# Second cross attention from halves, scores two rows ahead of the values; float8 weight quantised among the experts; rotary tables loaded and widened apart from the masks

## The chip, the core and the metric

One core of a Trainium2 chip runs the whole kernel in one launch. The metric is the device time in microseconds (us), lower is better. In the profile the engines are PE (TensorE matmuls), PEld (its weight loads), DVE (VectorE), ACT (ScalarE), POOL (GpSimd) and SPq (the queue of DMA issues of SyncE).

## The reference

The input x is 8 rows (batch) x 100 tokens x 512 features. Two decoder layers follow each other. Layer 0: a causal self attention with rotary positions (16 heads of 32), a cross attention to a context of 8 x 722 x 512, a mixture of 8 experts with three layers each. Layer 1: a self attention with a latent key and value, a second cross attention to the same context, and one 512 x 512 product with both factors rounded to float8. After each of the six parts the part's input is added and a layer norm taken. The parts that the change touches:

```
q, k = rope(q), rope(k)                     # layer 0: Y*cos + Y2*sin, tables by position
scores = einsum('bqh,bkh->bqk', q, k) * SCALE   # layer 1, second cross attention
attn = softmax(scores, axis=1)              # over the queries, not over the keys
out = einsum('bqk,bkh->bqh', attn, v)
k_q = (kernel / s_k).astype(float8_e4m3fn)  # layer 1, last product
```

## The kernel before

Each stage is a block in which every engine has its own list of instructions, in the order written, and waits on semaphores by hand. A stage ends when all engines have ended it. There is no planner.

**Front (`front_stage`, from L569).** The input rows x and the weights Wq, Wk, Wv, Wo are transposed on PE into PSUM banks, ACT keeps the high half of each result (rounded to fp32r, L693), DVE the low half (L731), and the projections of q and k are made of three products of halves. The list `FRONT` sets one order for all engines: four rows of x, the biases, four chunks of Wq, then sixteen "ropes" (a projected piece of 128 x 400), with the rest of x and of the weights between them. For a rope, PE projects, ACT adds the bias column (L702), POOL multiplies by the cosine table (L722), DVE swaps half heads (L738), multiplies by the widened sine table (L740) and adds (L744). POOL first issues 9 DMAs for biases (L714) and 13 for tables and masks (`rest`, L716: causal, turned_mask, own_chunk, enter, cos, sin, cos_q, sin_q, picks, spreads, gate_w, gate_b, iota8) and waits for all of `rest`. DVE calls `widen_tables` ahead of the low half of the first Wq chunk: it waits for all of `rest` too, then widens four masks (L748 to L751) and two sine tables (L753). SP clears the experts' rows in DRAM (14.8 MB, L626) once `rest` is there.

**Experts (L2035 to L2235).** 60 units (20 tiles x 3 layers) of 16 matmuls each, PE throughout. SP streams one weight of 1 MB per unit into six slots, with the last gathers and a list `last` of other loads between them. DVE has short work in two of three units.

**Second cross attention (`context_columns`, L1478).** Eight rows b, each with its context of 722 keys (6 tiles of 128, the last of 82). The context comes in two layouts: as columns (`ctx_ct`, 1444 KB a row, stored to DRAM by the first cross attention, `load_turned`) for the scores, and as rows in one of five buffers (`load_context`: one DMA of 5 x 128 keys, 1280 KB, and one of the 82 keys left, 164 KB) for the values. Per row: `scores(b)`, 24 float32 matmuls (L1513), keys on the partitions; DVE adds the key bias (L1580), reduces the maximum over the queries (L1586), ACT takes the exponent (L1552), DVE sums (L1596), inverts and multiplies (L1600), which gives `pT`; `value(b, c)`, 24 float32 matmuls with the context as the stationary operand (L1525), which gives the output already turned; 6 small matmuls (12 records) count the sums of `pT` (L1535). ACT copies the output (L1558), DVE the sums (L1606). On PE `scores(b + 1)` stands ahead of `value(b)`. DVE also does one of eight pieces of the float8 rounding of the last weight per row (`kernel_piece`, L2858 and L1171 to L1177). SP waits for scores(b - 2) ahead of the columns of row b; the rows of row b wait for value(b - 5).

The first cross attention (`context_rows`, L1189) already works from halves: ACT rounds the context rows to high halves (L1358), POOL makes the low ones (L1405), and each value is 18 matmuls of 512 columns (L1310).

## Time and profile before

| | us |
| --- | --- |
| median of 3 runs | 1012.65 (1008.77 to 1012.96) |
| the profiled execution: time | 1012.64 |
| the profiled execution: span in the trace | 1010.3 |
| mean granted TensorE clock, share of full | 0.951 |

PE is busy for 930.5 us of the span, DVE for 430.5, ACT for 346.4, POOL for 249.8. What lies around the span (2.3 us) is taken as fixed. A busy share is a mean over stages, so each stage is read in its own stretch: the front ends at about 72 us, the experts run from 447 to 681 us, the second cross attention from 850 to 942 us.

### The profile page before, as it was taken

Reading aid. Unit: us, or ns where it says so; the run is one execution under the profiler, and the core shown is the slowest. Engines: PE = TensorE matmul, PEld = TensorE weight load, DVE = VectorE, ACT = ScalarE, POOL = GpSimd, SP = SyncE. Lnnn points to the kernel's source line nnn. Section 1 sums busy time; section 2 is a strip of 40 time slices with the busy share of each in tenths; the row PEclk is TensorE's granted clock in tenths of the full one; section 3 lists DMA queues with packets and bytes.
Section 4 is the critical chain, followed back from the end, with each engine's and each line's share of the span. In section 5 each row is a group of like instructions: output and inputs, shape, how many; then the busy total and the mean of one; then the engine's idle time right before and its main releaser. Section 6 shows DMA issues by size and latency. Waiting matters only on the chain. (4 is left out here: it accounts for less than half of the span.)

```text
span 1010.3 us, 19157 instructions
## 1 busy us (share of the span) xinstructions
PE 930.5 (92%) x7712; PEld 750.3 (74%) x7712; DVE 430.5 (43%) x994; ACT 346.4 (34%) x886; POOL 249.8 (25%) x306
## 2 busy tenths in 40 slices
PE   3999999989998979999999999998978899999993
PEld 3987776577775643679999999996865568999531
DVE  2884443314443548001121133226257731555576
ACT  2332222234553123112233233325366621212374
POOL 4343111113555207000000000005056503000275
PEclk9999999999999969899999999997969999999996
DMA  9975000246731907049999888711050022972001
GB/s 258 382 257 189 2 2 2 68 128 223 249 138 62 339 1 257 12 140 389 357 382 340 278 272 281 257 39 55 1 156 3 2 96 89 325 241 76 1 14 51
DMA packets 72456, 162.01 MB, mean 160 GB/s; under 512 B 4132, under 2 KB 5685, under 8 KB 70321
## 3 DMA queue, kind: packets, MB, share of 16 engines
q1 hardware_dynamic: 70048, 156.54, 45.3%
q0 software_dynamic: 2320, 4.25, 1.4%
q8 instruction: 61, 1.00, 0.4%
q14 instruction: 27, 0.21, 0.1%
HBM read 128.81 MB, written 31.97 MB: 159 GB/s over the span
## 5 line engine op out<-in xcount | busy, mean ns | idle before, releaser
L2100 PE MATMUL ps<-ffn_h,ffn_w 128*128 128x128 f32 x1280 | 149.1, 275 | 0.0
L2100 PEld LDWEIGHTS ps<-ffn_h,ffn_w 128*128 128x128 f32 x1280 | 145.9, 192 | 0.0
L2100 PE MATMUL ps<-ffn_xh,ffn_w 128*128 128x128 f32 x640 | 74.9, 275 | 0.3 <-ACT ffn_xh L2134 0.3
L2190 DVE TENSOR_SCALAR ffn_h<-ps,tile_bias 128x128 f32<-128x128 f32 x80 | 22.5, 345 | 122.4 <-PE ps L2100 122.4
L2100 PEld LDWEIGHTS ps<-ffn_xh,ffn_w 128*128 128x128 f32 x640 | 73.1, 192 | 0.9 <-issue 0.9
L1405 POOL TENSOR_TENSOR ctx_low<-shelf,ctx_high 128x1024 fp32r<-128x1024 f32 (+2 forms) x24 | 43.0, 1821 | 65.4 <-PE ps L1270 33.7
L2148 ACT ACTIVATE ffn_y<-ffn_y 128x128 f32<-128x128 f32 x80 | 23.7, 298 | 73.9 <-DVE ffn_y L2206 73.9
L2206 DVE SCALAR_TENSOR_TENSOR ffn_y<-ps,tile_bias,ffn_gate_row 128x128 f32<-128x128 f32 x80 | 22.6, 345 | 58.0 <-PE ps L2100 57.9
L1513 PE MATMUL ps<-x_qT,ctx_ct 128*128 128x100 f32 (+1 forms) x384 | 44.8, 278 | 2.3 <-PEq L137 2.0
L1513 PEld LDWEIGHTS ps<-x_qT,ctx_ct 128*128 128x128 f32 (+1 forms) x384 | 43.3, 191 | 3.7 <-issue 3.2
L2818 POOL TENSOR_TENSOR att_e<-att_e,decay 100x400 f32<-100x400 f32 x32 | 32.7, 1033 | 45.8 <-DVE att_e L2669 45.8
L111 PE MATMUL ps<-ctx_ct,x_qT 128*100 128x210 f32 (+1 forms) x128 | 40.3, 467 | 1.0 <-DVE ctx_ct L1419 0.7
L2142 ACT ACTIVATE ffn_h<-ps,tile_bias 128x128 f32<-128x128 f32 x80 | 22.9, 368 | 41.6 <-PE ps L2100 41.6
L2987 POOL TENSOR_TENSOR rstd<-rstd,minus_half 100x1 f32<-100x1 f32 x16 | 11.7, 740 | 97.9 <-DVE rstd L2930 93.3
L111 PEld LDWEIGHTS ps<-ctx_ct,x_qT 128*100 128x100 f32 x128 | 20.6, 166 | 18.7 <-issue 17.4
L1525 PE MATMUL ps<-ctx_pT,shelf 128*128 128x100 f32 (+1 forms) x288 | 33.2, 275 | 0.2 <-ACT xf L1558 0.2
L2765 ACT ACTIVATE att_e<-att_e,att_mx 100x100 f32<-100x100 f32 x96 | 28.0, 366 | 15.4 <-DVE att_mx L2674 15.4
L1525 PEld LDWEIGHTS ps<-ctx_pT,shelf 128*128 128x128 f32 (+1 forms) x288 | 32.6, 192 | 0.4 <-issue 0.4
L1552 ACT ACTIVATE ctx_pk<-ctx_pk,ctx_st 128x100 f32<-128x100 f32 x48 | 13.8, 365 | 53.3 <-DVE ctx_st L1588 53.3
L2890 PE MATMUL ps<-x_n,xf 128*100 128x512 f32 x64 | 29.9, 596 | 0.6 <-PEq L1494 0.6
L111 PE MATMUL ps<-l_ro,xf 128*100 128x512 f32 x64 | 30.1, 615 | 0.0
L2134 ACT ACTIVATE ffn_xh<-ps 128x512 f32<-128x512 f32 x20 | 11.8, 598 | 49.0 <-PE ps L2061 49.0
(467 smaller groups left out, 2092.9 us busy)
## 6 DMA issues: line engine op xcount, KB each, us to landing
ffn_w<-in_L_ffn_w_dram SPq DMA_DIRECT2D x60, 1024.0 KB, 6.5
shelf<-in_ctx_dram SPq DMA_DIRECT2D x12, 1280.0 KB
expert_rows<-nothing SPq DMA_DIRECT2D x1, 14820.0 KB, 51.5
context_turned<-ctx_ct SPq DMA_DIRECT2D x8, 1444.0 KB, 7.9
ctx_ct<-context_turned SPq DMA_DIRECT2D x8, 1444.0 KB, 13.9
ctx_lent<-in_ctx_dram SPq DMA_DIRECT2D x4, 1280.0 KB
rows_own<-expert_rows SPq DMA_DIRECT2D x8, 260.0 KB, 3.0
x_wo<-in_L_xattn_Wo_dram SPq DMA_DIRECT2D x1, 2048.0 KB, 8.4
```

The costliest lines, as they stand in the source:

```text
L111: last = pe.matmul(out, a, b, start=(n == 0), stop=(n == len(products) - 1))
L1405: nc.gpsimd.tensor_tensor(raw_low[b % RAWS][0:rows_, j0:j1, :], raw[b % RAWS][0:rows_, j0:j1, :], raw_high[b % 2][0:rows_, j0:j1, :].bitca ...
L1513: mm = nc.tensor.matmul(ps[0:rows_, SB + i, (j - j0) * T:(j - j0 + 1) * T], ct[b % 2][:, k, j * P:j * P + rows_], qT[:, k, b * T:(b + 1) * T],
L1525: mm = nc.tensor.matmul(ps[:, VB, c * T:(c + 1) * T], raw[b % RAWS][0:keys(j), j, c * P:(c + 1) * P], pT[0:keys(j), b % 2, j, :], start=j ...
L2100: mm = nc.tensor.matmul(acc(n)[:, m, :], w[:, n % SLOTS, k, m * P:(m + 1) * P], into[l][:, i % 2, k, :], start=k == 0, stop=k == C - 1, sk ...
L2142: nc.scalar.activation(h1[:, i % 2, m, :], acc(n)[:, m, :], ACT.Relu, bias=bsel[:, m, i, 0:1]).then_inc(h1_kept, 1)
L2148: nc.scalar.activation(y[:, i % 2, m, :], y[:, i % 2, m, :], ACT.Relu, accum_out=vT[:, m, i:i + 1]).then_inc(counted, 1)
L2190: nc.vector.tensor_scalar(h2[:, i % 2, m, :], acc(n)[:, m, :], bsel[:, m, i, 1:2], 0.0, ALU.add, ALU.max).then_inc(h2_kept, 1)
L2206: nc.vector.scalar_tensor_tensor(y[:, i % 2, m, :], acc(n)[:, m, :], bsel[:, m, i, 2:3], gate_row[:, i % 2, :], ALU.add, ALU.mult).then_in ...
L2765: ins = nc.scalar.activation(e[:, c, :], e[:, c, :], ACT.Exp, bias=mx[:, b % 2, r, c:c + 1])
L2818: nc.gpsimd.tensor_tensor(e, e, decay[:, :].unsqueeze(1).to_broadcast([T, C, T]), ALU.mult).then_inc(faded, 1)
L2890: mm = nc.tensor.matmul(ps[0:T, b % 3, :], xf[:, k, b * T:(b + 1) * T], n1[:, k, :], start=k == 0, stop=False)
```

## The change

**Front.** The four rotary tables get a semaphore of their own and are issued ahead of the masks. POOL waits for them alone. DVE widens the sines at the first rope, and the masks (with the wait for `rest`) at rope 7.

```diff
         rest = [(causal_f, g["causal"]), (turned_f, g["turned_mask"]), (own_chunk[:, 0:C], g["own_chunk"]),
-                        (enter_f, g["enter"].rearrange("p (i r) t -> p i (r t)", i=2)), (cos[:], g["cos"]), (sin[:], g["sin"]), (cos_q[:], g["cos_q"]),
-                        (sin_q[:], g["sin_q"]), (picks[:], g["picks"]), (spreads[:], g["spreads"]),
+                        (enter_f, g["enter"].rearrange("p (i r) t -> p i (r t)", i=2)), (picks[:], g["picks"]), (spreads[:], g["spreads"]),
         in_rest = (in_rest[0], 16 * len(rest))
+        tables = [(sin_q[:], g["sin_q"]), (cos_q[:], g["cos_q"]), (sin[:], g["sin"]), (cos[:], g["cos"])]
+        in_tables = (nc.alloc_semaphore(name="in_tables"), 16 * len(tables))
...
                 def _(pool):
                     for dst, src in loads:
                         pool.dma_start(dst, src).then_inc(in_bias[0], 16)
+                    for dst, src in tables:
+                        pool.dma_start(dst, src).then_inc(in_tables[0], 16)
                     for dst, src in rest:
                         pool.dma_start(dst, src).then_inc(in_rest[0], 16)
-                    pool.wait_ge(*in_rest)
+                    pool.wait_ge(*in_tables)
...
-                    def widen_tables():
+                    def widen_masks():
                         dve.wait_ge(*in_rest)
...
+
+                    def widen_sines():
+                        dve.wait_ge(*in_tables)
                         for i, t in enumerate((sin_q, sin)):
-                            nc.vector.tensor_copy(by_batch(sines[:, i, :]), table(t)).then_inc(masked, 1)
-                        dve.wait_ge(masked, 6)
+                            nc.vector.tensor_copy(by_batch(sines[:, i, :]), table(t)).then_inc(widened, 1)
+                        dve.wait_ge(widened, 2)
...
                     for u in FRONT:
-                        if u == ("wq", 0):
-                            widen_tables()
+                        if u == ("rope", 0):
+                            widen_sines()
+                        if u == ("rope", 7):
+                            widen_masks()
```

On DVE, the front from the low halves of x on. Before:

```order
L731 TENSOR_TENSOR xT_lo<-ps,xT_hi 128x4x100 x4
L731 TENSOR_TENSOR l_bv_lo<-ps,l_bv_hi 128x4
L748 CAST causal<-k_roped 100x400
L750 CAST mask_and_max<-k_roped 128x400 x2
L751 CAST enter<-k_roped 128x400
L753 COPY rope_sines<-sin_q 128x400
L753 COPY rope_sines<-sin 128x400
L731 TENSOR_TENSOR l_wq_lo<-ps,l_wq_hi 128x512 x4
L738 STREAM_SHUFFLE rope_t_55<-rope_f 128x400
```

With the change:

```order
L734 TENSOR_TENSOR xT_lo<-ps,xT_hi 128x4x100 x4
L734 TENSOR_TENSOR l_bv_lo<-ps,l_bv_hi 128x4
L734 TENSOR_TENSOR l_wq_lo<-ps,l_wq_hi 128x512 x4
L759 COPY rope_sines<-sin_q 128x400
L759 COPY rope_sines<-sin 128x400
L741 STREAM_SHUFFLE rope_t_55<-rope_f 128x400
L743 TENSOR_TENSOR rope_t_55<-rope_t_55,rope_sines 128x400
L747 TENSOR_TENSOR q_roped<-rope_t_54,rope_t_55 128x400
```

The four mask casts are gone from ahead of the Wq low halves; the two sine copies stand behind them. The casts now stand in front of the rotation of rope 7.

**Float8 weight.** The load of the weight and of its scale moves from SP's list of the second self attention to the end of the experts' list; the eight pieces move to DVE's list in every second unit from unit 27 on.

```diff
+        in_kernel, k_step = nc.alloc_semaphore(name="in_kernel"), sem("kernel_step")
+        kernel_rows = kq[:].rearrange("p (c d) -> p c d", c=C)
+        PIECE_AT = {unit_at[10, 0] + 2 * b: b for b in range(B)}
+
+        def kernel_piece(dve, b):
+
+            v_, m_ = k_tmp[0][:], k_tmp[1][:]
+            piece = kq[:, b * PIECE:(b + 1) * PIECE]
+            steps = [lambda: nc.vector.tensor_scalar(v_, piece, sc_k[:, 1:2], None, ALU.mult)]
+            steps += float8_steps(piece, v_, m_)
+            for n, emit in enumerate(steps):
+                dve.wait_ge(k_step, len(steps) * b + n + 1)
+                emit().then_inc(k_step, 1)
+
...
-                        (rq, natural(g["L1_attn_Wq"]), in_qup)]
+                        (rq, natural(g["L1_attn_Wq"]), in_qup),
+                        (kernel_rows, natural(g["L1_ffn_kernel"]), in_kernel),
+                        (sc_k[:, 0:1], g["L1_ffn_kernel_scale"].partition_broadcast(P), in_kernel)]
...
+                    if n in PIECE_AT:
+                        b = PIECE_AT[n]
+                        if b == 0:
+                            dve.wait_ge(in_kernel, 32)
+                            nc.vector.reciprocal(sc_k[:, 1:2], sc_k[:, 0:1]).then_inc(k_step, 1)
+                        kernel_piece(dve, b)
```

**Second cross attention.** Values from halves, outputs turned back by PE, three buffers instead of five, scores two rows ahead.

```diff
-        RAWS = 5
+        RAWS, OWN_RAWS = 5, 3
...
-            raw = raws
+            raw = own_raws
+            raw_low = [sb_at(f"{name}_low{i}", [P, KT, D], shelf_at + 4 * KT * D * i, FR) for i in range(OWN_RAWS)]
+            raw_high = [sb_at(name + "_high0", [P, KT, D], xT_at, FR), sb(name + "_high1", [P, KT, D], FR, phase)]
+            pp = Pair(*(sb(f"{name}_pT_{half}", [P, 2, KT, T], FR, phase) for half in ("hi", "lo")))
+            an = sb(name + "_a", [T, 2, D], F32, phase)
...
                 @block.sync
                 def _(sp):
                     for b in range(2, B):
-                        if b >= RAWS:
-                            sp.wait_ge(used, b - RAWS + 1)
-                        load_context(sp, 1, b)
                         sp.wait_ge(scored, 2 * (b - 1))
                         load_turned(sp, b)
+                        if b >= OWN_RAWS:
+                            sp.wait_ge(used, b - OWN_RAWS + 1)
+                        load_context(sp, 1, b)
...
-                    def value(b, c):
-                        if c == 0:
-                            pe.wait_ge(even, b + 1)
-                            pe.wait_ge(landed[b % RAWS], 32 * (b // RAWS + 1))
-                            if b >= 1:
-                                pe.wait_ge(a_kept, b)
+                    def value(b):
+                        pe.wait_ge(low_p, b + 1)
+                        if b >= 1:
+                            pe.wait_ge(natural_a, b)
                         for j in range(KT):
-                            mm = nc.tensor.matmul(ps[:, VB, c * T:(c + 1) * T],
-                                                  raw[b % RAWS][0:keys(j), j, c * P:(c + 1) * P],
-                                                  pT[0:keys(j), b % 2, j, :], start=j == 0, stop=j == KT - 1,
+                            pe.wait_ge(low_raw, len(PIECES) * b + (j // 2 + 1 if j < KT - 1 else len(PIECES)))
+                            r = slice(0, keys(j))
+                            products = times(pp[r, b % 2, j, :], Pair(raw_high[b % 2], raw_low[b % OWN_RAWS])[r, j, :])
+                            for n, (p_, c_) in enumerate(products):
+                                mm = nc.tensor.matmul(ps[0:T, VB, :], p_, c_, start=j == 0 and n == 0,
+                                                      stop=j == KT - 1 and n == 2)
+                        mm.then_inc(used, 1)
+                        if b >= 1:
+                            pe.wait_ge(counted, b)
+                        for j in range(KT):
+                            group = j % HPC
+                            mm = nc.tensor.matmul(ps[group * HD:(group + 1) * HD, 5, 0:T], one[0:keys(j), :],
+                                                  pT[0:keys(j), b % 2, j, :], start=j < HPC, stop=j + HPC >= KT,
                                                   skip_group_check=True)
-                        if c == C - 1:
-                            mm.then_inc(used, 1)
-                            if b >= 1:
-                                pe.wait_ge(counted, b)
-                            for j in range(KT):
-                                group = j % HPC
-                                mm = nc.tensor.matmul(ps[group * HD:(group + 1) * HD, 5, 0:T], one[0:keys(j), :],
-                                                      pT[0:keys(j), b % 2, j, :], start=j < HPC, stop=j + HPC >= KT,
-                                                      skip_group_check=True)
-                            mm.then_inc(summed, 1)
+                        mm.then_inc(summed, 1)
...
+                    def turn_out(b):
+                        pe.wait_ge(natural_a, b + 1)
+                        if b >= 2:
+                            pe.wait_ge(out_kept, b - 1)
+                        for c in range(C):
+                            mm = nc.tensor.transpose(flip_bank(b)[:, c, :], an[:, b % 2, c * P:(c + 1) * P], ident[0:T, 0:T])
+                        mm.then_inc(flipped, 1)
 
                     scores(0)
+                    scores(1)
                     for b in range(B):
-                        if b + 1 < B:
-                            scores(b + 1)
-                        for c in range(C):
-                            value(b, c)
+                        if b + 2 < B:
+                            scores(b + 2)
+                        if b:
+                            turn_out(b - 1)
+                        value(b)
+                    turn_out(B - 1)
...
+                    def split(b, pieces):
+                        for i, rows_, j0, j1 in (PIECES[n] for n in pieces):
+                            if i == 0:
+                                act.wait_ge(landed[b % OWN_RAWS], 32 * (b // OWN_RAWS + 1))
+                                if b >= 2:
+                                    act.wait_ge(used, b - 1)
+                            nc.scalar.activation(raw_high[b % 2][0:rows_, j0:j1, :], raw[b % OWN_RAWS][0:rows_, j0:j1, :],
+                                                 ACT.Identity).then_inc(high_raw, 1)
...
-                    def keep_a(b):
+                    def high_of_p(b):
+                        act.wait_ge(even, b + 1)
+                        if b >= 2:
+                            act.wait_ge(used, b - 1)
+                        nc.scalar.activation(pp.hi[:, b % 2], pT[:, b % 2], ACT.Identity).then_inc(high_p, 1)
+
+                    def keep_natural(b):
                         act.wait_ge(used, b + 1)
-                        nc.scalar.activation(aT_out[:, :, b * T:(b + 1) * T],
-                                             ps[:, VB, 0:C * T].rearrange("p (c t) -> p c t", c=C),
-                                             ACT.Identity).then_inc(a_kept, 1)
-
+                        if b >= 2:
+                            act.wait_ge(flipped, b - 1)
+                        nc.scalar.activation(an[:, b % 2, :], ps[0:T, VB, :], ACT.Identity).then_inc(natural_a, 1)
+
+                    def keep_out(b):
+                        act.wait_ge(flipped, b + 1)
+                        nc.scalar.activation(aT_out[:, :, b * T:(b + 1) * T], flip_bank(b), ACT.Identity).then_inc(out_kept, 1)
+
+                    split(0, range(4))
                     expo(0)
+                    high_of_p(0)
+                    expo(1)
                     for b in range(B):
+                        if b:
+                            keep_natural(b - 1)
                         if b + 1 < B:
-                            expo(b + 1)
-                        keep_a(b)
+                            high_of_p(b + 1)
+                            split(b + 1, range(4))
+                        if b:
+                            keep_out(b - 1)
+                        if b + 2 < B:
+                            expo(b + 2)
+                    keep_natural(B - 1)
+                    keep_out(B - 1)
...
+                    def low_of_raw(b, pieces):
+                        for i, rows_, j0, j1 in (PIECES[n] for n in pieces):
+                            dve.wait_ge(high_raw, len(PIECES) * b + i + 1)
+                            nc.vector.tensor_tensor(raw_low[b % OWN_RAWS][0:rows_, j0:j1, :], raw[b % OWN_RAWS][0:rows_, j0:j1, :],
+                                                    raw_high[b % 2][0:rows_, j0:j1, :].bitcast(F32), ALU.subtract
+                                                    ).then_inc(low_raw, 1)
...
+                    low_of_raw(0, (0, 1))
                     shift(0)
+                    low_of_raw(0, (2, 3))
                     share(0)
+                    shift(1)
+                    low_of_p(0)
                     for b in range(B):
+                        if b:
+                            count(b - 1)
                         if b + 1 < B:
-                            shift(b + 1)
                             share(b + 1)
-                        beside(dve, b)
-                        count(b)
+                            low_of_p(b + 1)
+                            low_of_raw(b + 1, range(4))
+                        if b + 2 < B:
+                            shift(b + 2)
+                    count(B - 1)
```

On SP, the loads of the second cross attention (`ctx_ct` columns, 128x5x512 and 82x512 the rows). Before, from row 2 on:

```order
L781 DMA shelf<-in_ctx_dram 128x5x512
L783 DMA shelf<-in_ctx_dram 82x512
L2491 DMA ctx_ct_8799<-context_turned 128x2888
L781 DMA ctx_lent_838<-in_ctx_dram 128x5x512
L783 DMA ctx_lent_838<-in_ctx_dram 82x512
L2491 DMA ctx_ct_8800<-context_turned 128x2888
L781 DMA ctx_lent_839<-in_ctx_dram 128x5x512
L783 DMA ctx_lent_839<-in_ctx_dram 82x512
L2491 DMA ctx_ct_8799<-context_turned 128x2888
L781 DMA shelf<-in_ctx_dram 128x5x512
```

With the change:

```order
L2590 DMA ctx_ct_8936<-context_turned 128x2888
L790 DMA shelf<-in_ctx_dram 128x5x512
L792 DMA shelf<-in_ctx_dram 82x512
L2590 DMA ctx_ct_8937<-context_turned 128x2888
L790 DMA shelf<-in_ctx_dram 128x5x512
L792 DMA shelf<-in_ctx_dram 82x512
L2590 DMA ctx_ct_8936<-context_turned 128x2888
L790 DMA shelf<-in_ctx_dram 128x5x512
L792 DMA shelf<-in_ctx_dram 82x512
L2590 DMA ctx_ct_8937<-context_turned 128x2888
```

The columns of a row now stand ahead of its rows. Each load of rows from row 3 on (the second 128x5x512 of the list after) waits for value(b - 3), and the columns of the row after it are queued behind that wait.

On DVE, one row in the middle of that stage. Before (the eight `k_quant` and `kernel` instructions are a piece of the float8 weight):

```order
L1580 TENSOR_TENSOR ctx_pk<-ps,x_qbk 128x500
L1580 TENSOR_TENSOR ctx_pk<-ps,x_qbk 82x100
L1586 TENSOR_REDUCE ctx_st<-ctx_pk 128x6
L1588 TENSOR_SCALAR ctx_st<-ctx_st 128x6
L1596 TENSOR_REDUCE ctx_st<-ctx_pk 128x6
L1598 RECIPROCAL ctx_st<-ctx_st 128x6
L1600 TENSOR_TENSOR ctx_pT<-ctx_pk,ctx_st 128x600
L2858 TENSOR_SCALAR k_quant<-kernel,s_k 128x256
```

With the change:

```order
L1652 TENSOR_REDUCE ctx_st<-ctx_pk 128x6
L1654 RECIPROCAL ctx_st<-ctx_st 128x6
L1656 TENSOR_TENSOR ctx_pT<-ctx_pk,ctx_st 128x600
L1664 TENSOR_TENSOR ctx_pT_lo<-ctx_pT,ctx_pT_hi 128x600
L1674 TENSOR_TENSOR ctx_low_10662<-shelf,ctx_high_10663 128x1024 x2
L1674 TENSOR_TENSOR ctx_low_10662<-shelf,ctx_high_10663 128x512
L1674 TENSOR_TENSOR ctx_low_10662<-shelf,ctx_high_10663 82x512
L1636 TENSOR_TENSOR ctx_pk<-ps,x_qbk 128x500
L1636 TENSOR_TENSOR ctx_pk<-ps,x_qbk 82x100
L1642 TENSOR_REDUCE ctx_st<-ctx_pk 128x6
```

The low halves of the probabilities and of four pieces of the context now stand on DVE between the share of a row and the shift of the next.

## Rows read from the trace of the kernel before

**Rows 1.** Windows: stretch, PE, PEld, DVE, ACT, POOL busy (count), PEclk, DMA share, GB/s.

```profile
24.20:27.70 3.50, 3.50 (x11) 3.47 (x12) 0.00 (x0) 0.00 (x0) 0.00 (x0) 0.50 1.05 392
45.00:55.00 10.00, 10.00 (x62) 9.81 (x61) 9.68 (x20) 3.76 (x7) 4.23 (x4) 1.00 1.06 378
580.00:620.00 40.00, 40.00 (x361) 40.00 (x361) 13.40 (x38) 13.53 (x50) 2.83 (x3) 1.00 0.84 281
```

**Rows 2.** Timeline of the front: start, length, engine, instruction [idle before <-releaser].

```profile
7.71 0.77 POOL L716 DMA_DIRECT2D k_roped<-in_enter_dram  x1
...
17.30 1.22 ACT L693 ACTIVATE l_wq_hi<-ps 128x512 fp32r<-128x512 f32 x2 [0.26 <-PE ps L645]
19.77 0.37 DVE L748 CAST causal<-k_roped 100x400 fp32r<-100x400 f32 x1 [4.86 <-DMA iota<-in_iota_dram]
...
24.20 0.67 PE L111 MATMUL ps<-xT_hi,l_wq_hi 128*128 128x400 f32 x1 [6.31 <-DVE l_wq_lo L731]
...
28.92 0.61 DVE L738 STREAM_SHUFFLE rope_t<-rope_f 128x400 f32<-128x400 f32 x1
```

**Rows 3.** DMA issues: KB each, us from issue to landing.

```profile
sin_q<-in_sin_q_dram POOLq DMA_DIRECT2D x1, 50.0 KB, 6.5
```

**Rows 4.** Timeline of the second cross attention, one row of it.

```profile
917.83 0.94 DVE L1580 TENSOR_TENSOR ctx_pk<-ps,x_qbk 128x500 f32<-128x500 f32 x2 [2.45 <-PE ps L1513]
918.31 5.52 PE L1525 MATMUL ps<-ctx_pT,shelf 128*128 128x100 f32 x48
...
919.83 1.72 ACT L1552 ACTIVATE ctx_pk<-ctx_pk,ctx_st 128x100 f32<-128x100 f32 x6 [6.60 <-DVE ctx_st L1588]
...
922.62 0.78 DVE L1600 TENSOR_TENSOR ctx_pT<-ctx_pk,ctx_st 128x600 f32<-128x600 f32 x1
923.32 0.35 DVE L2858 TENSOR_SCALAR k_quant<-kernel,s_k 128x256 f32<-128x256 bf16 x1
...
923.77 0.54 PE L1535 MATMUL ps<-ctx_pT,ctx_one 128*32 128x100 f32 x12
...
924.24 5.39 PE L1513 MATMUL ps<-x_qT,ctx_ct 128*128 128x100 f32 x48
...
926.27 0.26 DVE L1606 COPY x_sums<-ps 128x100 f32<-128x100 f32 x1
```

**Rows 5.** Timeline of the first cross attention, turned output, values and halves.

```profile
262.65 0.51 PE L1278 MATMUL ps<-ident,ctx_a 100*128 100x100 f32 x4
...
263.47 0.40 PE L1310 MATMUL ps<-ctx_high,ctx_pT_lo 128*100 128x512 f32 x1
...
263.70 0.39 PE L1310 MATMUL ps<-ctx_high,ctx_pT_hi 128*100 128x512 f32 x1
...
265.52 2.00 ACT L1358 ACTIVATE ctx_high<-ctx_lent 128x1024 fp32r<-128x1024 f32 x2
```

**Rows 6.** Lines: DVE subtracting halves, both operands in SBUF, mean ns of one.

```profile
L1873 DVE TENSOR_TENSOR x_wq_lo<-x_wq,x_wq_hi 128x512 fp32r<-128x512 f32 x8 | 4.9, 687 | 0.0
```

**Rows 7.** SP's queue, the issue of one load of columns.

```profile
873.89 0.85 SPq L2491 DMA_DIRECT2D ctx_ct<-context_turned  x1
```

**Rows 8.** Landing of the columns issued at 823.96, 873.89, 896.20 and 907.35.

```profile
ctx_ct<-context_turned SPq DMA_DIRECT2D x1, 1444.0 KB, 6.2
...
ctx_ct<-context_turned SPq DMA_DIRECT2D x1, 1444.0 KB, 13.9
...
ctx_ct<-context_turned SPq DMA_DIRECT2D x1, 1444.0 KB, 15.5
...
ctx_ct<-context_turned SPq DMA_DIRECT2D x1, 1444.0 KB, 14.7
```

**Rows 9.** Windows as rows 1, around and in the second cross attention.

```profile
848.00:850.00 2.00, 0.03 (x2) 0.06 (x1) 0.00 (x0) 0.59 (x1) 0.05 (x1) 1.00 0.00 0
850.40:853.80 3.40, 3.40 (x19) 3.40 (x18) 0.00 (x0) 0.00 (x0) 3.40 (x4) 0.50 0.81 232
...
918.00:921.00 3.00, 3.00 (x31) 3.00 (x29) 1.72 (x4) 1.17 (x5) 0.00 (x0) 1.00 0.10 43
```

More of the change, by code:

```diff
@@ L1635, in program @@
         decay = sb("decay", [T, T], F32, late)
+        PIECE = C * D // B
+        uzp = pair("x1_uz", [P, C], late)
+        kq, sc_k = sb("kernel", [P, C * D], BF16, late), sb("s_k", [P, 4], F32, late)
         turned_at = shelf_at + 4 * OWN * XW
         rk, rv = (sb_at("l1_raw_" + n, [P, C, D], turned_at + 4 * C * D * i) for i, n in enumerate("kv"))
+        k_tmp = [sb_at(f"k_quant{i}", [P, PIECE], turned_at + 4 * 2 * C * D + 4 * PIECE * i) for i in range(2)]
         rq_at = TOP - 4 * C * D
@@ L2049, in _ @@
                         to, src, landed = last.pop(0)
-                        sp.dma_start(to if to is rw else to[:], src).then_inc(landed, 16)
+                        sp.dma_start(to if to is rw or landed is in_kernel else to[:], src).then_inc(landed, 16)
                 for s in range(SLOTS):
```

52 lines of the change are left out of this document (23 added, 29 removed).

## Prediction

> **What bounds the kernel now.** I read the table of windows first: PE is at work nearly all the time, so the end is set stage by stage by how long PE is kept there, and by what keeps it waiting. Among the experts PE is busy 40.00 of 40 us and DVE 13.40 [rows 1]; there only PE counts. Then the timeline of the front. PE stands idle for 6.31 us until 24.20, released by the low halves of Wq, and DVE makes those so late because it stood 4.86 us, until 19.77, for the last DMA of the tables and masks [rows 2]. After that idle time PE runs at 0.50 of its clock for 3.5 us [rows 1]. From about 29 us to the end of the front (45 to 55 us in rows 1 shows it) DVE is busy 9.68 of 10 us, with semaphore gaps of some 0.03 us between its instructions, and PE is full as well: DVE sets the pace and has no slack.
>
> In the second cross attention a row takes PE 11.15 us: 5.46 for values and 0.46 for the sums of the probabilities (918.31 to 923.77 to 924.24), 5.15 for scores plus a handshake [rows 4]. DVE has its chain of one row under it, with 2.45 us of idle time. The landing times tell the rest: a load of columns that is alone lands after 6.2 us, but in this stage after 13.9 to 15.5 [rows 8]. The two loads of a row (1444 KB of columns, 1444 KB of rows) are never finished when the next pair is issued. Before, this costs nothing: from the issue of a row's columns to their use PE works on two values and one score, about 16.5 us.
>
> **The front.** The tables now stand in the issue slots of the masks, up to about 8.5 us [rows 2], and land 6.5 us later [rows 3], at 15: before they are wanted. DVE can follow ACT's last high half of Wq (end 18.52 [rows 2]) with one subtraction of 0.69 [rows 6], so PE starts at 19.3 instead of 24.20: 4.9 us. PE then has been idle 1.4 us instead of 6.3; if the clock stays, the 3.5 us at half clock become 1.75: another 1.7. Back come the four mask casts, 0.37 each [rows 2] and partly overlapped, 1.2 us together, on a DVE without slack ahead of rope 7. Net gain 5.5 us. Bounds: 3.8 if the clock falls in the short idle time too, 6.7 if the casts find room. The front is followed by attention that waits for none of the loads still running (clearing of the experts' rows), so I let all of it through. The clearing keeps its start: it waits for the same last DMA.
>
> **The float8 pieces.** One takes DVE 2.95 us (923.32 to 926.27 less a copy [rows 4]). Among the experts PE needs 3.8 us per unit and DVE has 27 of 40 us free [rows 1]; results wait three units in their bank ring. In the worst unit (short work 1.1 us, then a piece) DVE comes 0.3 us late to the next unit, which PE wants two units later. Cost 0; without that cover it would be 8 x 2.95. In the stage they leave they had cover as well (idle 2.45 us per row), so leaving gains nothing by itself. The weight's load (512 KB) joins a queue at 281 GB/s while PE never waits: 0.
>
> **Second cross attention, PE alone.** 18 products of 512 columns at a pitch of 0.23 us (263.47 to 263.70 [rows 5]) are 4.15 us, in place of 5.46; turning the output back costs some 0.35 (busy 0.51, overlapped [rows 5]). A row becomes 5.15 + 0.35 + 4.15 + 0.46 = 10.1 us: 1.05 less, 8.4 in eight rows. This is what PE would give; I do not expect to see it, for two reasons.
>
> **First, the loads.** The change gives three row buffers for five, so the rows of b wait for value(b - 3), and the columns of b + 1 are queued behind that wait on SP. They are wanted at scores(b + 1), one row of PE later: 10.1 + 0.5 us. The pair takes longer. The columns issued at 873.89, 896.20 and 907.35 landed at 887.8, 911.7 and 922.05 [rows 7, 8]; that is 23.9 us for two pairs and 10.35 for the last one, 11.4 each, with the queue never empty. Started from nothing a pair needs the start-up too, 1.8 us (6.2 less 4.4, an estimate for 1444 KB at a little under the 378 GB/s of [rows 1]). The chain over two rows is pair 11.4 + 1.8, then scores 5.15, turn 0.35, values 4.15: 22.9, or **11.4 us per row**, not 10.1. For what makes a pair slow there is a row: at 918 to 921 the load moves 43 GB/s at a DMA share of 0.10 [rows 9], that is 1.6 of 16 engines, while the other engines have ended.
>
> The Trainium skill (DMA: Bandwidth & Descriptors, "Why a DMA increments its semaphore by 16 and not by 1") says that a DMA is spread over the largest number of engines up to 16 that divides its partitions. For the load of 82 keys that is 2: 82 KB on each of two engines, beside 80 + 90 KB which every engine has of a pair. By equal shares a pair would take some 8.5 us and hide under 10.1; by the rule two engines carry a pair and a half. The trace agrees, with 43 GB/s at the end.
>
> **Second, DVE and ACT.** Now they form a loop, since DVE must end its low halves before it shifts the next scores: exponent 1.72, share 1.77 (two of 0.78 and a reciprocal), high half of the probabilities 0.67 (estimate between ACT's sizes), first piece of the context on ACT 1.0 (2.00 for two [rows 5]), four low halves on DVE 3.5 (3072 columns by 687 ns per 512 less overlap [rows 6]), shift and maximum 1.85, handshakes 0.3: 10.8 us. It too is above 10.1.
>
> **The stage.** It starts at 850 at half clock (3.4 us after 2.0 idle [rows 9]): scores(0) ends at 857, scores(1) at 862.6. Scores(2) now stand ahead of value(0), and their columns, issued at 857.0, come at 863.7; value(0) ends at 873. Five rows at 11.4 take value(5) to 930.1; two more values without scores, 2 x 5.0, and 2.2 of waits for ACT's copies bring 942.3; the last output goes copy, turn, copy where it went copy: 1.6. That is 943.9 against 942: +1.9. PE then idles 1.3 us per row in uneven portions, and idle times of 2.0 us have been followed by half clock for 3.4 us [rows 9], 1.7 us of work each. I count one and a half of these: +2.6. Together **+4.5**.
>
> **Sum.** 1012.64 (profiled execution, equal to the median 1012.65) - 5.5 + 4.5 = 1011.6; I say **1011.5**. A measurement of this kernel can tell some 0.5% (5 us) from no change.
>
> **Rivals.** (a) *The loads keep up*, since half of the pairs follow a drained queue, and the DVE and ACT loop sets 10.8: the stage ends at 943, +1: 1008.1. For it: the last pair took 10.35. Against: the mean of 11.4. (b) *PE sets the pace* at 10.1: 873 + 50.5 + 13.8 = 937, -5, so 1002. It needs both a faster DVE and faster loads; nothing in the rows shows either. (c) *Slower: PE at half clock in most rows of the second cross attention.* If the uneven idle times reach about 1.6 us in most rows, each is followed by half clock: 5 falls x 1.7 = 8.5 on the +1.9, and pairs at 11.95 each, as between 887.8 and 911.7, add 0.55 / 2 x 5 = 1.4: +11.8, and the front's short idle time costs its 1.7 (gain 3.8): 1012.6 - 3.8 + 11.8 = 1020.6. It decides from a chain of about 12 us per row. (d) *The front does not give it*: x rows 4 to 7 are now wanted at 21.5 instead of 28, behind Wq (landed 13.9) in a saturated queue; if they landed at 24 the gain shrinks by 2.5: 1014.
>
> **Chances.** Forecast 0.45, (a) 0.22, (b) 0.08, (c) 0.17, (d) 0.08. Half of (a) and all of (b) pass the bound of 1007.6 for faster, with 0.05 of the forecast's own width: 0.24. Slower than 1017.7: (c) and a little of (d) with late loads: 0.20. The same: 0.56. The range leaves out most of (b) and the far half of (c): 1004.5 to 1018.5.
>
> **What would show it.** Front: PE's first Wq product at 19 to 20 us, the clock at 1.00 through it, the first rotation near 22, the first attention some 5.5 us earlier. Experts: PE still without idle time. Second cross attention: 18 products at 0.23 us; PE idle ahead of the scores of rows 3 to 7 with the columns' DMA as releaser, landings of 12 to 13 us after the issue, distance of values 11 to 12 us; the stage some 94 us long instead of 92. Wrong I would be if values follow each other at 10.1 to 10.8 without such waits, or if PE's first product still comes after 21.

## The result, and the profile after

| | before | after |
| --- | --- | --- |
| median, us (11 runs each, same chip) | 1012.16 (1007.25 to 1013.76) | 1016.25 (1009.95 to 1018.67) |
| ratio to before | | 1.0052, 95% interval 1.0034 to 1.0071 |
| profiled execution: time, span | 1012.64, 1010.3 | 1017.42, 1015.6 |
| mean granted clock | 0.951 | 0.948 |

The change made the kernel slower by half a per cent. The forecast was 1011.5, about 1 us less than the kernel before, with the range up to 1018.5: the direction was wrong.

**The front gave what was forecast.** Timeline of the changed kernel's front, as rows 2:

```profile
6.64 0.55 POOL L717 DMA_DIRECT2D cos_q<-in_cos_q_dram  x1
...
19.21 0.69 DVE L734 TENSOR_TENSOR l_wq_lo<-ps,l_wq_hi 128x512 fp32r<-128x512 f32 x1 [0.16 <-ACT l_wq_hi L694]
19.82 0.36 DVE L759 COPY rope_sines<-sin_q 128x400 f32<-128x400 f32 x1
20.05 0.42 PE L111 MATMUL ps<-xT_hi,l_wq_hi 128*128 128x400 f32 x1 [1.51 <-DVE l_wq_lo L734]
20.30 0.34 PE L111 MATMUL ps<-xT_lo,l_wq_hi 128*128 128x400 f32 x1
20.48 0.34 PE L111 MATMUL ps<-xT_hi,l_wq_lo 128*128 128x400 f32 x1
```

DVE's last low half of Wq now stands ahead of the sines, and PE starts at 20.05, after 1.51 us of idle time and not 6.31 [rows 2]. From the second on its products follow each other at 0.18 us, which is full speed. The first scores of attention:

```profile
73.81 0.96 PE L856 MATMUL ps<-k_roped,q_roped 32*100 32x100 f32 x32
```

before, and of the changed kernel:

```profile
68.05 0.96 PE L865 MATMUL ps<-k_roped,q_roped 32*100 32x100 f32 x32
```

That is 5.8 us earlier. The second cross attention starts 4.9 us earlier (849.97, now 845.06).

**The experts did not notice the float8 pieces.** Windows, columns as rows 1, of the changed kernel:

```profile
580.00:620.00 40.00, 40.00 (x361) 40.00 (x360) 24.49 (x69) 15.68 (x60) 1.12 (x4) 1.00 0.85 272
882.80:889.60 6.80, 6.80 (x32) 6.80 (x33) 5.18 (x7) 4.71 (x9) 0.00 (x0) 0.50 0.95 359
891.50:896.00 4.50, 4.50 (x29) 3.02 (x29) 1.13 (x3) 2.27 (x8) 0.00 (x0) 1.00 0.09 39
910.00:917.00 7.00, 6.97 (x33) 7.00 (x34) 4.21 (x5) 2.77 (x4) 0.00 (x0) 0.51 0.89 309
```

In the first of them DVE went from 13.40 to 24.49 us, and PE is still busy for 40 of 40. From the first to the last product of the experts PE takes 229.99 us in both kernels.

**The second cross attention lost it.** From its first product of scores to the next stage's first product it took 92.38 us (849.97 to 942.35) and now takes 102.74 (845.06 to 947.80): +10.4. Timeline of the changed kernel, from the issue of columns 4 to scores(6) (L1529 scores, L1543 values, L1550 sums):

```profile
869.78 0.33 SPq L2590 DMA_DIRECT2D ctx_ct<-context_turned  x1
...
879.82 0.54 PE L1550 MATMUL ps<-ctx_pT,ctx_one 128*32 128x100 f32 x12
882.78 1.57 PE L1529 MATMUL ps<-x_qT,ctx_ct 128*128 128x100 f32 x6 [2.43 <-DMA ctx_ct<-context_turned]
...
896.33 5.39 PE L1529 MATMUL ps<-x_qT,ctx_ct 128*128 128x100 f32 x48
...
901.85 0.45 PE L1543 MATMUL ps<-ctx_high,ctx_pT_hi 128*100 128x512 f32 x1
902.14 0.40 PE L1543 MATMUL ps<-ctx_low,ctx_pT_hi 128*100 128x512 f32 x1
902.38 0.39 PE L1543 MATMUL ps<-ctx_high,ctx_pT_lo 128*100 128x512 f32 x1
...
910.03 8.62 PE L1529 MATMUL ps<-x_qT,ctx_ct 128*128 128x100 f32 x48 [3.30 <-DMA ctx_ct<-context_turned]
```

PE stands idle 2.43 us ahead of scores(4) and 3.30 ahead of scores(6), each time for the columns, and each time the scores that follow run at half clock (0.50 and 0.51 in the windows) and take 8.6 us, not 5.4. In between, values run as forecast: steps of 0.23 us. Landing of the columns issued at 869.78, 880.77 and 896.81, in the DMA view, which answer to rows 8:

```profile
ctx_ct<-context_turned SPq DMA_DIRECT2D x1, 1444.0 KB, 12.9
...
ctx_ct<-context_turned SPq DMA_DIRECT2D x1, 1444.0 KB, 15.2
...
ctx_ct<-context_turned SPq DMA_DIRECT2D x1, 1444.0 KB, 13.1
```

With the one issued at 907.14 (13.9) they land at 882.7, 896.0, 909.9 and 921.0: a pair of loads every 12.8 us on average. And ahead of a landing (891.5 to 896.0 above) the load moves 39 GB/s at a share of 0.09, as in [rows 9].

### The profile page after: what moved, and what is told of

Its sections match the earlier page's. It is cut to its first block and busy times, and to the rows that moved or that the text cites. A ratio compares the mean times of both kernels' runs of the same rounds, so it can differ in the third digit from the quotient of the medians.

```text
span 1015.6 us, 18861 instructions
## 1 busy us (share of the span) xinstructions
PE 929.4 (92%) x7504; PEld 736.7 (73%) x7504; DVE 466.7 (46%) x1034; ACT 379.7 (37%) x934; POOL 252.0 (25%) x306
## 5 line engine op out<-in xcount | busy, mean ns | idle before, releaser
L1529 PE MATMUL ps<-x_qT,ctx_ct 128*128 128x100 f32 (+1 forms) x384 | 51.2, 302 | 10.2 <-DMA ctx_ct<-context_turned 5.7
L1529 PEld LDWEIGHTS ps<-x_qT,ctx_ct 128*128 128x128 f32 (+1 forms) x384 | 49.8, 215 | 11.8 <-issue 8.7
L2240 ACT ACTIVATE ffn_h<-ps,tile_bias 128x128 f32<-128x128 f32 x80 | 22.9, 368 | 41.7 <-PE ps L2198 41.7
L1674 DVE TENSOR_TENSOR ctx_low<-shelf,ctx_high 128x1024 fp32r<-128x1024 f32 (+2 forms) x32 | 30.7, 1020 | 2.0 <-ACT ctx_high L1581 2.0
L1353 ACT ACTIVATE ctx_ct<-ps 128x512 f32<-128x512 f32 x24 | 14.2, 597 | 41.0 <-PE ps L1279 41.0
L111 PE MATMUL ps<-x_woT,x_wv 128*128 128x512 f32 x64 | 27.7, 594 | 0.0
```

Of the source, the lines that this page charges most:

```text
L111: last = pe.matmul(out, a, b, start=(n == 0), stop=(n == len(products) - 1))
L1529: mm = nc.tensor.matmul(ps[0:rows_, SB + i, (j - j0) * T:(j - j0 + 1) * T], ct[b % 2][:, k, j * P:j * P + rows_], qT[:, k, b * T:(b + 1) * T],
L1674: nc.vector.tensor_tensor(raw_low[b % OWN_RAWS][0:rows_, j0:j1, :], raw[b % OWN_RAWS][0:rows_, j0:j1, :], raw_high[b % 2][0:rows_, j0:j1, ...
L2240: nc.scalar.activation(h1[:, i % 2, m, :], acc(n)[:, m, :], ACT.Relu, bias=bsel[:, m, i, 0:1]).then_inc(h1_kept, 1)
```

## The experiments

Each kernel was timed against the kernel before on the same chip. The medians of before were 1012.16 (beside front_only, old_columns, order and tail), 1011.98 (hold, order_tail, order_shift, order_shift_tail) and 1010.88 (hold2, shift, before_tail, front_place), so kernels of different groups are compared by their ratios. "Stage" is from the first product of scores to the next stage's first product; "row" is a quarter of the time from value(1) to value(5).

| kernel | median | ratio to before, 95% interval | stage | row |
| --- | --- | --- | --- | --- |
| before | 1012.16 | | 92.38 | 11.15 |
| after | 1016.25 | 1.0052 (1.0034, 1.0071) | 102.74 | 13.40 |
| front_only | 1004.59 | 0.9934 (0.9908, 0.9961) | 92.38 | 11.15 |
| old_columns | 1005.88 | 0.9940 (0.9918, 0.9962) | 92.37 | 11.15 |
| front_place | 1006.60 | 0.9962 (0.9944, 0.9980) | 92.37 | 11.15 |
| before_tail | 1012.34 | 1.0009 (0.9988, 1.0031) | 92.38 | 11.15 |
| order | 1008.54 | 0.9971 (0.9954, 0.9989) | 95.32 | 10.67 |
| tail | 1010.01 | 0.9983 (0.9962, 1.0003) | 95.29 | 10.67 |
| order_tail | 1010.04 | 0.9998 (0.9978, 1.0018) | 95.32 | 10.67 |
| hold | 1015.51 | 1.0041 (1.0021, 1.0062) | 102.39 | 13.31 |
| hold2 | 1014.91 | 1.0047 (1.0024, 1.0070) | 100.26 | 12.88 |
| shift | 1014.69 | 1.0040 (1.0022, 1.0058) | 100.65 | 13.11 |
| order_shift | 1002.37 | 0.9919 (0.9892, 0.9946) | 89.80 | 10.32 |
| order_shift_tail | 1001.66 | 0.9914 (0.9887, 0.9941) | 89.39 | 10.33 |

The expectations count a stage to a product that comes later, one that is not the same in both forms of the kernel: their 96.7 of before is 92.4 here, their 106.2 and 98.8 are 102.7 and 95.3. Differences between kernels of the changed form are not touched by that. The time of whole kernels is a coarser gauge: the ones with the new front reach the stage anywhere between 839.7 and 845.7 us, and even those with the same program up to there (the change, order, tail, hold and their like) spread from 839.7 to 845.5.

**Which part costs.** front_only is the kernel before with the front's lines of the diff; old_columns is the changed kernel with context_columns of before, without its float8 pieces.

> The kernel before with the front's part of the change alone (tables first, masks cast later). Theory A (the trace of the change: first attention 5.8 us earlier, of which 4.9 are left at the second cross attention): 1007 to 1008, ratio to before 0.995. Rival B (what comes earlier is given back in a wait or at half clock further on, as the stages between gave back 0.9): no difference, 1011 to 1013.

> The changed kernel with the second cross attention of before (five row buffers, float32 values, no float8 pieces beside it; those stay among the experts). Theory A (the stage alone costs, the float8 pieces cost 0): as the kernel with the front's part alone, 1007 to 1008. Rival B (the pieces in the experts, or the weight's load there, cost something; or their leaving the stage gives something): 2 us or more away from it, in either direction.

Both gain 6 to 7 us by their ratios, somewhat more than theory A had, and they do not differ by more than their intervals of some 2.5 us. The traces are sharper: the experts take 229.99 us from first to last product with the pieces among them (old_columns) and without (front_only). So the front gives the gain, the float8 pieces cost nothing, and the new second cross attention alone turns a gain of 0.6% into a loss of 0.5%.

**Where the wait comes from.** order issues the columns of row b + 1 on SP before it waits for value(b - 3):

```diff
-    for b in range(2, B):
-        sp.wait_ge(scored, 2 * (b - 1))
-        load_turned(sp, b)
-        if b >= OWN_RAWS:
-            sp.wait_ge(used, b - OWN_RAWS + 1)
-        load_context(sp, 1, b)
+    sp.wait_ge(scored, 2)
+    load_turned(sp, 2)
+    load_context(sp, 1, 2)
+    for b in range(3, B):
+        if b == 3:
+            sp.wait_ge(scored, 4)
+            load_turned(sp, 3)
+        if b + 1 < B:
+            sp.wait_ge(scored, 2 * b)
+            load_turned(sp, b + 1)
+        sp.wait_ge(used, b - OWN_RAWS + 1)
+        load_context(sp, 1, b)
```

> The changed kernel; the columns of row b+1 are issued ahead of the wait for value(b-3), not behind it. Theory A (the columns came late since they stood behind that wait, and each wait was followed by half clock): no wait of scores for the columns, the columns then land 15 us before use; the two waits (2.4 and 3.3) and 6.4 us of half clock go, less what the rows' loads cause when they come later in turn: 3 to 9 us less than the change, 1007 to 1013. Rival B (the loads' total rate binds: 11.4 us per pair in any order): the wait moves to the rows (ACT's high halves with the shelf's DMA as releaser, PE idle before values), and at most 2 us are gained. Rival C (DVE and ACT's loop of 10.8 us sets the row): no DMA wait at all, rows of 10.8, 8 us less.

tail makes one load into two, in this stage alone (the wait for a row's loads then counts 48 and not 32):

```diff
-    sp.dma_start(raws[slot][0:LAST, KT - 1, :], g["ctx_1024"][b, whole:S, :]).then_inc(landed, 16)
+    sp.dma_start(raws[slot][0:80, KT - 1, :], g["ctx_1024"][b, whole:whole + 80, :]).then_inc(landed, 16)
+    sp.dma_start(raws[slot][80:LAST, KT - 1, :], g["ctx_1024"][b, whole + 80:S, :]).then_inc(landed, 16)
```

> The changed kernel; the load of 82 keys is made as one of 80 and one of 2. Theory A (82 rows fall on 2 of 16 engines, which makes a pair of loads 11.4 us): a pair takes 8.5 to 9.5 us, columns land 9 to 10 us after their issue where it was 13.0, the two waits of scores go, 6 to 9 us less than the change. Rival B (the pair is slow for another reason, such as rows of 2 KB or the queue's turn-over): landings of 13 us as now, and no difference in time.

Either edit takes 7.4 us off the stage, and all waits for columns with it, as theory A had for each. The rows of 10.67 us are what order's theory C expected. In the waits view of order, over the stage, PE's waits within it are

```profile
PE ps L1566 <- ACT ctx_a L1607: 4.0, 3, 3.5
PE ps L1535 <- DVE ctx_pk L1642: 3.6, 7, 1.5
```

(total, times, longest), where the changed kernel had

```profile
PE ps L1529 <- DMA ctx_ct<-context_turned: 5.7, 2, 3.3
```

In tail the columns issued at 866.22, 877.22 and 887.93 land after 9.5, 9.5 and 10.0 us where it was 13 to 15. Two windows up to such a landing (886.7), columns as rows 1, of tail:

```profile
884.00:885.50 1.50, 1.50 (x9) 1.03 (x8) 1.50 (x3) 1.27 (x3) 0.00 (x0) 1.00 0.98 416
885.50:886.70 1.20, 1.20 (x15) 0.69 (x15) 1.20 (x3) 0.00 (x0) 0.00 (x0) 1.00 0.03 10
```

The thin end of the load is gone: it runs at 416 GB/s until about a microsecond before it has landed. Nothing but the split of 82 partitions into 80 and 2 was changed. The prediction cites the Trainium skill (DMA: Bandwidth & Descriptors, "Why a DMA increments its semaphore by 16 and not by 1") for the rule that a DMA goes over the largest number of engines, up to 16, that divides its partitions. The traces agree with it: with 82 partitions a load ends at a share of 0.09 to 0.10, which is 1.4 to 1.6 of 16 engines, and with 80 and 2 it runs at 0.98 nearly to its end.

> Both of the load edits together: columns issued ahead of the wait, and the load of 82 keys made as 80 and 2. Theory A (with either edit alone the rows of the stage already follow each other at 10.7 us, which is the loop of DVE and ACT): nothing further, the stage again 98.8 us, 1008 to 1010. Rival B (loads still cost part of the 10.7): rows of 10.3 us, 3 us less.

Both together give no more than either: 95.32 us, rows of 10.67. What is left is not the loads.

> The kernel before with the load of 82 keys made as 80 and 2. Theory A (the two engines' load is slow there too, but hidden behind 16.5 us of work): columns land after 9 to 10 us instead of 13.9 to 15.5, the stage stays 96.7 us and the time 1011 to 1013. Rival B (the load's two engines cost the kernel before something as well): 2 us or more less.

The kernel before hid its slow load altogether: its stage stays at 92.38. But the split was worth more there than I expected: the columns issued at 896.62 and 907.78 land after 6.0 and 5.9 us, where it was 15.5 and 14.7 [rows 8]. That is as quick as the load that is alone (6.2 [rows 8]), so nothing of the rows is left in the queue when the columns come.

**What is left: DVE and ACT.** shift and order_shift move one call on DVE, in the changed kernel and in order:

```diff
     low_of_p(b + 1)
-    low_of_raw(b + 1, range(4))
 if b + 2 < B:
     shift(b + 2)
+if b + 1 < B:
+    low_of_raw(b + 1, range(4))
```

> Columns issued ahead of the wait, and on DVE the shift and maximum of scores(b+2) stand ahead of the low halves of the context of row b+1, not behind them. Theory A (the loop shift, exponent, share, high and low half of the probabilities, low halves of the context, shift sets 10.67 us per row, and at the end keeps PE idle for 3.5 us ahead of turning out row 5): rows of about 10.3 us, no wait of PE for ctx_pk, and no idle time of 3.5 us at the end; the stage some 93 us instead of 98.8, the time 1003. Rival B (the low halves come late for values and PE waits there instead): rows of 10.7 or more, no gain. Rival C (rows of 10.3 us are too quick for the loads, 11.4 us a pair): a DMA wait returns, with half clock, and up to 5 us of the gain with it.

> The changed kernel with nothing but the shift and maximum of scores(b+2) ahead of the low halves of the context on DVE; the columns stay behind the wait for value(b-3). Theory A (the loads set the row there, DVE and ACT have slack): the stage within 1.5 us of the change's 106.2, the time 1015 to 1017, though the same edit gave 5.5 us of stage once the columns were issued earlier. Rival B (the loop of DVE and ACT is part of the chain of the loads): 3 us or more less.

The loop is plain in the timeline of order, DVE and ACT over one row:

```profile
892.98 0.78 DVE L1662 TENSOR_TENSOR ctx_pT<-ctx_pk,ctx_st 128x600 f32<-128x600 f32 x1
893.80 0.70 ACT L1601 ACTIVATE ctx_pT_hi<-ctx_pT 128x600 fp32r<-128x600 f32 x1 [1.41 <-DVE ctx_pT L1662]
894.41 3.03 ACT L1587 ACTIVATE ctx_high<-shelf 128x1024 fp32r<-128x1024 f32 x4
895.48 3.56 DVE L1680 TENSOR_TENSOR ctx_low<-shelf,ctx_high 128x1024 fp32r<-128x1024 f32 x4 [0.17 <-ACT ctx_high L1587]
898.96 0.84 DVE L1642 TENSOR_TENSOR ctx_pk<-ps,x_qbk 128x500 f32<-128x500 f32 x2
```

DVE never stands free between the low halves (3.56) and the shift, and PE waits 0.3 us per row for that shift. At the end of the stage it costs more: ACT's exponent of row 7 stands ahead of its copy of output 5, and PE waits 3.5 us.

```profile
922.19 1.72 ACT L1593 ACTIVATE ctx_pk<-ctx_pk,ctx_st 128x100 f32<-128x100 f32 x6 [3.03 <-DVE ctx_st L1650]
923.82 0.57 ACT L1607 ACTIVATE ctx_a<-ps 100x512 f32<-100x512 f32 x1
924.44 0.56 PE L1566 MATMUL ps<-ident,ctx_a 100*128 100x100 f32 x4 [3.52 <-ACT ctx_a L1607]
```

After that wait the granted clock is 0.50 from 925.1 to 928.4. With the shift first, the rows take 10.32 us, the long wait at the end is 1.2 with no fall of the clock behind it, and the stage 89.80 instead of 95.32. That version is faster than both kernels. In the changed kernel itself the same edit gave 2.1 us, a little more than theory A allowed: one of the two falls of the clock became shorter (3.5 us, where it was 7), while the waits for columns stayed (3.14 and 3.11 us). Why one fall lasts 3.5 us and another 7 is open.

> The edits of columns ahead of the wait, of the shift ahead of the low halves, and of 80 and 2 keys, together. Theory A (nothing is left but PE's own work): rows of 10.3 us, the stage 93 us, the time 1002 to 1003, faster than the kernel before by 9 us. Rival C (if the loads held back the kernel without the 80 and 2): this one is faster than that one by 2 us or more.

0.4 us less in the stage than without the 80 and 2, and no difference in time that can be told. It is the fastest version found, with 1001.66 us.

**What the clock costs.** hold and hold2 give PE products into an unused bank while it waits; the diff is that of hold2, and hold has {4: 5, 6: 7} in the first line:

```diff
+    for n in range({4: 3, 5: 2, 7: 5}.get(b, 0)):
+        nc.tensor.matmul(ps[0:T, 2, 0:4 * T], qT[:, 0, 0:T], qT[:, 1, 0:4 * T], start=True, stop=True)
     pe.wait_ge(came[b % 2], 16 * (b // 2 + 1))
```

> The changed kernel with work for PE where it waits for the columns: 5 products of 400 columns in float32 into an unused bank ahead of scores(4) (2.2 us by the 0.112 us per 100 columns of the scores), 7 ahead of scores(6) (3.1 us). Their results are used by nobody; nothing is left out. Theory A (the stage's extra time is in half the clock's fall after each wait, on the chain columns, scores, values, rows, columns): the clock stays at 1.00, scores(4) and scores(6) take 5.4 us and not 8.6, the stage is some 6 us shorter than in the change although PE does more, and the time 1010. Rival B (the wait itself is what costs, and the clock's fall is absorbed by the next wait for loads): no gain, 1016, or 5 us slower than the change if the products come on top.

Scores(4) and (6) ran at full clock and took 5.3 us, and the stage was 0.35 us shorter. The wait went on to scores(5) (1.89 us, half clock for 3.5 us), and the products outlasted the waits: one took 0.72 us, where I had counted 0.45. Theory A fell; rival B, that the next wait absorbs the fall, came nearer. hold2 mends the sizes.

> The changed kernel with PE kept at work in its waits for columns, with less of it than in the kernel with 5 and 7 products, where these overran the landings by 1.3 and 4.8 us (one of 400 columns took 0.72 us): 3 ahead of scores(4), 2 ahead of scores(5), 5 ahead of scores(7). Theory A, as it stands after that run (a pair of loads of 82 and more keys takes 11.5 to 14 us and sets the row, about 13 us; the slow scores after a wait shorten the next wait, so the clock costs little by itself): columns land 12 to 14 us apart as before, the stage 104 to 105 us against 106.2, the time 1014 to 1016. Rival B (half the stage's extra time is the clock): the stage 100 us, 1010.

Waits view of hold2 over the stage, and its window from 849, at the end of scores(0), to the last value:

```profile
PE ps L1531 <- DMA ctx_ct<-context_turned: 2.6, 2, 1.4
```

```profile
849.00:945.00 96.00, 88.31 (x657) 70.47 (x656) 64.56 (x103) 48.00 (x100) 8.81 (x6) 1.00 0.55 186
```

The granted clock is 1.00 throughout that window, and the stage is only 2.5 us shorter than in the change (up to 1.6 more is in the last filling, which outlasted its wait). Columns land at 882.8, 895.9, 907.7 and 919.9: 12.4 us apart. A slow scores(4) cost little because scores(5) would have waited 1.9 us for its columns anyway. So the falls cost some 2.5 to 4 us, and the loads the rest.

**Which part of the front gives it.** front_place has the casts where the change puts them, and the tables where before has them in the queue. Its difference from front_only:

```diff
-    for dst, src in tables:
+    for dst, src in rest[:4]:
+        pool.dma_start(dst, src).then_inc(in_rest[0], 16)
+    for dst, src in reversed(tables):
         pool.dma_start(dst, src).then_inc(in_tables[0], 16)
-    for dst, src in rest:
+    for dst, src in rest[4:]:
         pool.dma_start(dst, src).then_inc(in_rest[0], 16)
     pool.wait_ge(*in_tables)
+    pool.wait_ge(*in_rest)
...
     dve.wait_ge(*in_tables)
+    dve.wait_ge(*in_rest)
```

> The kernel before with the casts moved as in the change (sines at the first rotation, masks at rotation 7), but with the tables among the masks in the order of issue as before, and all waits for all of them. Theory A (what held PE was DVE's wait standing ahead of the low halves of Wq; where the tables stand in the queue hardly matters, since the last of them had landed by 19.77 and the first rotation is at 22): the same as with the whole front, 1004 to 1006. Rival B (the order of issue is what gives the time): 3 us or more slower than that.

PE started at 19.02 us (18.80 in front_only) after 1.50 us of idle time: the place of the casts is what releases it, as theory A says. Timeline of front_place:

```profile
19.82 0.54 PE L111 MATMUL ps<-xT_hi,l_wq_lo 128*128 128x400 f32 x1
20.04 0.37 DVE L763 COPY rope_sines<-sin_q 128x400 f32<-128x400 f32 x1 [1.16 <-DMA iota<-in_iota_dram]
20.16 0.54 PE L111 MATMUL ps<-xT_hi,l_wq_hi 128*128 128x400 f32 x1
```

DVE still waits for the last mask, now for 1.16 us and with nobody behind it. As a whole kernel it gains 0.38% where front_only gains 0.66%: some 3 us less, with intervals that overlap. So the times do not exclude rival B, that the order of issue gives part of the gain. The trace has a reason for 1.7 us that need not be the order of issue: here the first twelve products take 3.74 us, at 0.33 us each, and in front_only 2.08, at 0.18. Kernels with one and the same front differ by as much (below).

## Why the prediction was wrong

- **Front.** Right, with some luck. Forecast -5.5, bounds -3.8 to -6.7; measured 5.8 us at the first attention, and -0.66% (6.7 us) as a whole kernel. The clock stayed in the profiled execution of the change, as taken. In six of the twelve traces with the new front it did not: there PE's first products run at half pace and the first attention comes 3.8 to 5.3 us earlier than in the trace of before, where the other six have 5.8 to 6.9. Those are about the two bounds of the forecast. Rival (d), late rows of x, did not come: PE's products run on.
- **Float8 pieces.** Right: 0. The experts take 229.99 us in every kernel, to 0.01.
- **PE alone in the stage.** Near: 10.1 us per row forecast; 10.32 measured once nothing else bound it. The stage was then 2.6 us shorter than before, where the forecast's rival (b) had 5.
- **DVE and ACT's loop.** Right: 10.8 forecast, 10.67 measured in order and tail. What I had too small was the end: the two last values took 8.7 and 7.0 us from one to the next, with a wait of 3.5 us and 3.4 us at half clock in them, not 5.0 plus 2.2 of waits for both, so this loop alone makes the stage 2.9 us longer than before, not 1.
- **The loads.** This is the step that failed: "the chain over two rows is pair 11.4 + 1.8, then scores 5.15, turn 0.35, values 4.15: 22.9, or 11.4 us per row". The chain is there, and its term of 11.4 us for a pair was too small. It was a mean. The columns issued at 885.04 landed at 899.1 in the kernel before, so the last three pairs took 11.3, 12.6 and 10.4 us, and the middle one is what the changed kernel was to see. A pair queued on a queue not yet empty, which I gave 11.4 without start-up, took 13.3 us (882.7 to 896.0), and 12.4 on average in hold2, where no fall of the clock stands between. The start-up was too small as well: 1444 KB at the 378 GB/s named there take 3.9 us (an estimate), so the load of 6.2 us leaves 2.3 and not 1.8. Rows came to 13.40 us with the falls and to 12.88 without them (hold2), of which up to 0.4 is the filling that outlasted its wait. From 11.4 to 12.5 or 12.9 in four rows are 4.3 to 5.9 us.
- **The same chain, read over two rows.** From the landing of columns 4 to that of columns 6 it takes 27.2 us (882.7 to 909.9) where I had 22.9: scores at half clock took 8.4 and not 5.15, and the pair 13.9 from the issue of its rows (895.96) and not 13.2. This looks like the clock. But in hold2, with scores(4) at full clock, the same distance is still 24.9 us (882.8 to 907.7), since the pair now waits for the one ahead of it, and two pairs of 12.4 are 24.8.
- **The clock.** Forecast +2.6 as one and a half falls of 1.7; there were two of 3.2 us each (8.6 less 5.4), and about half of that was swallowed by the next wait for loads. Its net, 2.5 to 4 us, is about what I had said, which is luck in part: fewer and shorter falls were forecast, and nothing of them swallowed.
- **Sum.** 92.4 + 1.9 + 2.6 was forecast for the stage, 102.7 measured: 5.8 too little. Of this 5.4 are in the four rows from value(1) to value(5), which took 53.6 us where 45.6 and 2.6 for the clock were forecast. The pair accounts for 4.3 to 5.9, and what may be left is the clock. Against the stage's 10.4 the front had 4.9 left at its start, and that is the slowdown. Rival (c), to which I gave 0.17, had a stage this slow ("It decides from a chain of about 12 us per row"), but not by this mechanism: it counted five falls of the clock and 1.4 us for the pairs, and there were two falls, with the pairs as the larger part.

Why a pair needs 12.4 to 13.3 us and not 11.4 in this stage is not settled. What makes it slow as a whole is: with 80 and 2 keys instead of 82 columns land 9.5 to 10.0 us after their issue.

## What to carry to other kernels

When a change puts a wait in front of a queue's next load, take the load's time from the worst pair in the trace (12.6 us here) and not from the mean (11.4), and ask what else stands behind that wait: moving one issue ahead of it was worth 7.4 us of stage here, more than the 2.6 to 3.0 us that the new form saved in the end. Look at the partitions of each load: the end of the load of 82 ran at a DMA share of 0.1, which is 1.6 of 16 engines, and cutting it into 80 and 2 removed that. And after the first bound is lifted, run again: here three stood behind each other, loads (7.4 us with the clock), DVE's order (5.5), and only then PE.

## What the runs showed of the hardware

- A load of 82 partitions holds up the columns queued behind it: in the kernel before they landed after 14.7 us, and after 5.9 with the load split into 80 and 2.
- A wait that is partly filled on PE can keep the clock at 1.00: hold2 had no fall after scores(0), where the changed kernel had two of 7 us. In this stage no idle time of PE from 1.2 to 1.54 us was followed by half clock, in any of the runs; those of 1.89 to 3.5 us all were, for 3.4 to 7 us.
- A granted clock of 1.00 in a window can be a missing record. In front_place the window 20 to 22 us shows PEclk 1.00, as in front_only, after the same idle time (1.50 and 1.54 us):

```profile
20.00:22.00 2.00, 2.00 (x8) 1.98 (x7) 0.65 (x2) 0.00 (x0) 0.00 (x0) 1.00 1.04 366
```

and front_only:

```profile
20.00:22.00 2.00, 2.00 (x14) 1.77 (x13) 0.02 (x2) 0.74 (x2) 0.00 (x0) 1.00 1.04 378
```

Yet the one makes 8 products in 2 us and the other 14. The first record of the clock in the trace of front_only is at 16.8 us, and in that of front_place at 22.7, which is where its products go from a distance of 0.33 us to one of 0.18. Ahead of its first record a window shows 1.00 only because nothing says otherwise. The same holds for old_columns, hold2, shift, order_shift and tail (first records at 22.4 to 25.3 us, distance 0.33 until then), while the changed kernel, order, hold, order_tail and order_shift_tail have theirs at 17.1 to 19.2 and a distance of 0.18 from the start. Most of these have the same program up to this point, so the program does not decide it. No run here shows what does. The distance between products is the surer sign.
